# Moving the MLP's second product, the maximum pass, a norm and two tanh between the stages of a 16-batch attention and mixture-of-experts kernel

## The reference

```python
xn = layernorm(x)                                # plain, no gain
# branch 1: attention, a linear recurrence and an MLP
h  = layernorm(xn) * ln1_g + ln1_b
q, k, v = heads(h @ WQ + bQ), heads(h @ WK + bK), heads(h @ WV + bV)   # 16 heads of 8
scores = q @ k.T / sqrt(8); masked to 0 <= i - j < 128
ao = softmax(scores) @ v
states = scan(s = A * s + (h @ Bw)_t)
g  = sigmoid(h @ Wg + bg)
x1 = xn + g * (ao @ WO + bO) + (1 - g) * (states @ Cw)
s  = x1 + gelu(layernorm(x1) @ W1 + b1) @ W2 + b2
# branch 2: a mixture of 8 experts, 2 per token
xc = bfloat16(xn); nf = rmsnorm(xc) * norm_weight
w  = softmax over the two largest of (nf @ gate_weight.T + gate_bias)
y  = sum over experts e of w_e * expert_e(nf)    # clamped gated unit, then a second product
out = x + s * silu(xc + y)
```

## Time and profile before

| what | value |
|---|---|
| median of 3 runs | 1091.38 us (1089.91 to 1097.93) |
| time of the profiled execution | 1094.57 us |
| its span | 1092.8 us |
| TensorE matmul busy | 919.2 us, 84% of the span |
| VectorE busy | 782.5 us, 72% |
| ScalarE busy | 712.8 us, 65% |
| GpSimd busy | 501.8 us, 46% |
| mean granted TensorE clock | 0.925 of full speed |

### The profile page before, as it was taken

The page is one execution under the profiler, slowest core; times in us unless marked ns, Lnnn a source line. Parts: engine busy times, 40 slices in busy tenths (PEclk is TensorE's granted clock), DMA queues, the critical chain, the costliest instruction groups (busy, mean ns, idle before and its releaser), DMA issues.

```text
span 1092.8 us, 38402 instructions
## 1 busy us (share of the span) xinstructions
PE 919.2 (84%) x15864; PEld 561.7 (51%) x15864; DVE 782.5 (72%) x1990; ACT 712.8 (65%) x1126; POOL 501.8 (46%) x786
## 2 busy tenths in 40 slices
PE   2567898989889898988889898989888898978877
PEld 1333564646455464645555464645555464635435
DVE  4476777887877677888777777887777788656216
ACT  3205685858677595858768595867768585746645
POOL 6226355372736356273626456273635547152331
PEclk7557999999999899999999999998999999978869
DMA  5552414123332404224241503223241402310000
GB/s 108 129 118 67 93 46 105 32 94 64 100 62 75 90 27 108 50 90 62 92 75 53 112 24 109 52 90 63 75 93 36 111 17 99 58 31 6 25 1 10
DMA packets 85599, 75.24 MB, mean 69 GB/s; under 512 B 9329, under 2 KB 79154, under 8 KB 85426
## 3 DMA queue, kind: packets, MB, share of 16 engines
q1 hardware_dynamic: 83346, 72.00, 28.3%
q10 hardware_dynamic: 2080, 0.79, 0.3%
HBM read 36.33 MB, written 30.15 MB: 61 GB/s over the span
## 4 chain that ended last, share of the span: by engine, by line
PE 48%; DVE 25%; issue 13%; ACT 9%; POOL 2%; DMA 2%; DVEq 0%; SPq 0%; POOLq 0%; ACTq 0%
PE ps L558 8%; DVE mx L1074 6%; PE ps L500 6%; PE ps L690 5%; PE ps L750 5%; PE ps L711 5%; ACT pt L831 4%; PE ps L489 3%; DVE gc L1131 3%; PE ps L570 2%; DVE lin L1124 2%; PE ps L575 2%; ACT ot L836 2%; DVE junk L950 2%; PE ps L684 2%
## 5 line engine op out<-in xcount | busy, mean ns | idle before, releaser
L831 ACT ACTIVATE pt<-ps 128x1024 f32<-128x1024 f32 (+1 forms) x256 | 234.7, 917 | 212.5 <-PE ps L489 211.1
L1074 DVE TENSOR_REDUCE mx<-ps 128x2 f32<-128x320 f32 (+1 forms) x512 | 230.9, 466 | 110.6 <-PE ps L515 107.6
L1253 POOL TENSOR_SCALAR_AFFINE_SELECT pt<-pt 128x512 f32<-128x512 f32 x256 | 170.7, 669 | 264.6 <-ACT pt L831 264.3
L500 PE MATMUL ps<-kd,qz 48*32 48x160 bf16 (+1 forms) x4096 | 160.5, 241 | 66.6 <-DVE mx L1074 34.2
L489 PE MATMUL ps<-qz,kd 51*32 51x256 bf16 (+1 forms) x4096 | 183.5, 272 | 6.1 <-ACT pt L831 3.8
L558 PE MATMUL ps<-pt,va 128*32 128x256 f32 (+1 forms) x2048 | 159.8, 397 | 33.2 <-ACT ot L836 33.0
L500 PEld LDWEIGHTS ps<-kd,qz 48*32 48x32 bf16 x4096 | 72.7, 91 | 218.7 <-issue 121.3
L690 PEld LDWEIGHTS ps<-m,act_t 128*128 128x128 f32 x1024 | 126.8, 191 | 53.6 <-DVE act_t L1152 38.6
L690 PE MATMUL ps<-m,act_t 128*128 128x128 f32 x1024 | 143.2, 283 | 11.6 <-DVE act_t L1152 11.6
L1256 POOL TENSOR_SCALAR_AFFINE_SELECT pt<-pt 128x512 f32<-128x512 f32 x192 | 124.6, 649 | 0.0
L879 ACT ACTIVATE lin<-ps,mbias 128x512 f32<-128x512 f32 x128 | 87.7, 685 | 48.7 <-DVE act_t L1152 29.5
(11 more groups left out here) (158 smaller groups left out, 1672.7 us busy)
## 6 DMA issues: line engine op xcount, KB each, us to landing
qz<-qk_parts SPq DMA_DIRECT2D x32, 384.0 KB, 7.3
...
```

The lines of the kernel that those rows point to most:

```text
L500: nc.tensor.matmul(ps[QG * c:QG * (c + 1), 4 + par, w * pr:w * (pr + 1)], qz[q][rows, 2 * g + pr, P * i + QG * c:P * i + QG * (c + 1)], kd ...
L831: nc.scalar.activation(to, src, ACT.Exp, scale=SCALE).then_inc(exp_ok.sem, 1)
L1074: nc.vector.tensor_reduce(mx[:, i, HG * g + pr:HG * (g + 1):2], src, AX.X, ALU.max).then_inc(mx_ok.sem, 1)
L1253: sel1 = nc.gpsimd.affine_select(out=pt[:, s, :, 0:P], in_=pt[:, s, :, 0:P], compare_op=ALU.is_ge, fill=0.0, base=0, pattern=[[0, HG], [1, ...
```

## The change

`LEAD = 2`: a step n of the attention loop now computes the transposed scores of batch b at n, as before, but the maximum scores of batch b + 1 at n + 2. The maximum scores of steps 0 and 1 of a batch are computed at the end of the body before (`first_scores` on TensorE, `maxima` at the end of VectorE's body, behind z). nm is formed at step 14 and turned and copied at step 15, within the loops.

The MLP's second product isn't computed behind the last expert any more, but in the next body: half of it (`mlp_down`) behind the scores of step 0, half behind those of step 1, in front of the states product, which moves from step 0 to step 1. sres is formed in VectorE's step 5, `finish` moves from steps 1 and 3 to 7 and 9, and GpSimd's ob from step 2 to step 5.

`norm_x` moves from ScalarE to VectorE, as `(xl - mean) * r1`, ahead of z, so GpSimd's `minus` for it goes. `norm_h` moves from the end of ScalarE's body to steps 0 and 1 of the next. The two tanh move from the start of ScalarE's body behind the exponentials of steps 2 and 3. nmT's copy moves to step 15, which is ahead of the second tiny activation at step 16. The first two parts of `route_mix` move from steps 9 and 11 to 11 and 13.

```diff
-AT_STATES, AT_H0, AT_Q, AT_K, AT_U, AT_V, AT_G, AT_C = 0, 2, 4, 6, 8, 10, 12, 14
+LEAD = 2
+AT_STATES, AT_H0, AT_Q, AT_K, AT_U, AT_V, AT_G, AT_C = 1, 2, 4, 6, 8, 10, 12, 14
 AT_CAST, AT_SQ, AT_RS, AT_NF = 4, 6, 8, 10
 AT_H2 = 4
-MIX = (9, 11, 15, 16)
+MIX = (11, 13, 15, 16)
...
-        r1_step = signal("r1_step", 4)
+        r1_step = signal("r1_step", 2)
         r2_step = signal("r2_step", 4)
-        xn_ok = signal("xn_ok", NT)
+        xn_ok = signal("xn_ok", 2)
...
             def scores(b, q, n, half):
-                main, nxt = has(b), has(b + 1)
-                if main and half == 0:
-                    if n == 0:
+                main, nxt = has(b) and n < NCH, has(b + 1) and n + LEAD < NCH
+                if main:
+                    if n == 0 and half == 0:
                         pe.wait_ge(*done(stacks_in, b))
                         pe.wait_ge(*done(shift_in, b))
                         pe.wait_ge(*done(hid_ok, b - 1))
-                    if n >= 2:
+                    if half == 0 and n >= 2:
                         pe.wait_ge(*done(exp_ok, b, n - 1))
-                if main and half == 1 and n >= 1:
-                    pe.wait_ge(*done(exp_ok, b, n))
+                    if half == 1 and n >= 1:
+                        pe.wait_ge(*done(exp_ok, b, n))
                 if nxt:
-                    if n == 0 and half == 0:
-                        pe.wait_ge(*done(stacks_in, b + 1))
-                        pe.wait_ge(*done(gc_ok, b - 1, E))
-                    else:
-                        pe.wait_ge(*done(mx_ok, b + 1, 2 * n - 1 + half))
+                    maxima_free(b + 1, n + LEAD, half)
                 for pr in range(2):
                     if nxt:
-                        score(b + 1, 1 - q, n, half, pr)
+                        score(b + 1, 1 - q, n + LEAD, half, pr)
                     if main:
                         mm = score_t(b, q, n, 1 - half, pr)
                 if main and half == 1:
                     mm.then_inc(sT_ps.sem, 1)
                 if nxt:
-                    score_mask(n, half)
+                    score_mask(n + LEAD, half)
+            def maxima_free(b, n, half):
+                if n == 0 and half == 0:
+                    pe.wait_ge(*done(stacks_in, b))
+                    pe.wait_ge(*done(gc_ok, b - 2, E))
+                else:
+                    pe.wait_ge(*done(mx_ok, b, 2 * n - 1 + half))
+            def first_scores(b, q, n, half):
+                maxima_free(b, n, half)
+                for pr in range(2):
+                    score(b, q, n, half, pr)
+                score_mask(n, half)
...
+                def mlp_down(t):
+                    pe.wait_ge(*done(hid_ok, b - 1))
+                    for j in range(NJ):
+                        mm = nc.tensor.matmul(bank_t(6)[:, t], hid[:, j, P * t:P * (t + 1)], w2[:, j], start=j == 0, stop=j == NJ - 1)
+                    if t == NT - 1:
+                        mm.then_inc(w2_ps.sem, 1)
...
+                    if has(b - 1) and n < 2:
+                        mlp_down(2 * n)
+                        mlp_down(2 * n + 1)
                     if main and n == AT_STATES:
...
+                    if nxt and n == NCH - LEAD + 1:
+                        pe.wait_ge(*done(nm_step, b + 1))
+                        for t in range(NT):
+                            mm = nc.tensor.transpose(bank_bf(5)[0:NPART * H, P * t:P * (t + 1)], nm[:, t].rearrange("p r h -> p (r h)"), identb[:])
+                        mm.then_inc(nm_ps.sem, 1)
...
                     down(E - 1)
-                    for t in range(NT):
-                        for j in range(NJ):
-                            if t == 0:
-                                pe.wait_ge(*done(hid_ok, b, j + 1))
-                            mm = nc.tensor.matmul(bank_t(6)[:, t], hid[:, j, P * t:P * (t + 1)], w2[:, j], start=j == 0, stop=j == NJ - 1)
-                    mm.then_inc(w2_ps.sem, 1)
...
+                if nx2:
+                    if start(b, -2):
+                        all_set(pe)
+                        pe.wait_ge(masks_set.sem, N_MASKS)
+                    for n in range(LEAD):
+                        for half in range(2):
+                            first_scores(b + 2, q, n, half)
...
-                def norm_x(t):
-                    act.wait_ge(*done(r1_step, b + 3))
-                    act.wait_ge(*done(xn_copied, b + 1))
-                    nc.scalar.activation(xn[:, 1 - q, t], xl[:, 1 - q, t], ACT.Identity, bias=b1n[:, t:t + 1],
-                                         scale=r1[:, t:t + 1]).then_inc(xn_ok.sem, 1)
                 def norm_h(t):
-                    act.wait_ge(*done(r2_step, b + 3))
-                    act.wait_ge(*done(xn_ok, b + 3, t + 1))
-                    act.wait_ge(*done(hT_ps, b + 2))
-                    nc.scalar.activation(h0[:, t], xn[:, 1 - q, t], ACT.Copy, scale=r2[:, t:t + 1]).then_inc(h0_ok.sem, 1)
+                    act.wait_ge(*done(r2_step, b + 2))
+                    act.wait_ge(*done(xn_ok, b + 2))
+                    act.wait_ge(*done(hT_ps, b + 1))
+                    nc.scalar.activation(h0[:, t], xn[:, q, t], ACT.Copy, scale=r2[:, t:t + 1]).then_inc(h0_ok.sem, 1)
...
+                    if nx2 and n < 2:
+                        norm_h(2 * n)
+                        norm_h(2 * n + 1)
+                    if has(b - 1) and n == 2:
+                        soft_gate()
+                    if nxt and n == 3:
+                        mix_gate()
+                    if nxt and n == NCH - LEAD + 1:
+                        act.wait_ge(*done(nm_ps, b + 1))
+                        act.wait_ge(*done(shift_in, b))
+                        nc.scalar.activation(nmT[:], bank_bf(5)[0:NPART * H, :], ACT.Copy).then_inc(nmT_ok.sem, 1)
...
+            def norm_x(b, q, tiles):
+                if tiles[0] == 0:
+                    dve.wait_ge(*done(r1_step, b))
+                    dve.wait_ge(*done(xn_copied, b - 2))
+                for t in tiles:
+                    ts = nc.vector.tensor_scalar(xn[:, q, t], xl[:, q, t], mv[:, t, 0:1], r1[:, t:t + 1], ALU.subtract, ALU.mult)
+                ts.then_inc(xn_ok.sem, 1)
+            def maxima(b, n, pr):
+                g, i = n // NT, n % NT
+                w = WIN if i else P
+                dve.wait_ge(*done(s_ps, b, 2 * n + pr + 1))
+                if n == 0 and pr == 0:
+                    dve.wait_ge(*done(nm_step, b - 1))
+                src = bank(4 + pr)[:, 0:2 * w].rearrange("p (r k) -> p r k", r=2)
+                nc.vector.tensor_reduce(mx[:, i, HG * g + pr:HG * (g + 1):2], src, AX.X, ALU.max).then_inc(mx_ok.sem, 1)
...
+                        if nxt and n + LEAD < NCH:
+                            maxima(b + 1, n + LEAD, pr)
+                        if has(b - 1) and step == 5:
+                            dve.wait_ge(*done(w2_ps, b - 1))
+                            dve.wait_ge(*done(x1b_ok, b - 1))
+                            dve.wait_ge(*done(ob_ok, b - 2))
+                            nc.vector.tensor_tensor(sres[:], bank_t(6), x1b[:], ALU.add).then_inc(s_ok.sem, 1)
+                        if has(b - 1) and step in (7, 9):
+                            finish(b - 1, (step - 7) // 2)
...
-                    if nxt and n == NCH:
+                    if nxt and n == NCH - LEAD:
...
+                if nx3:
+                    norm_x(b + 3, 1 - q, (0, 1))
+                    norm_x(b + 3, 1 - q, (2, 3))
                 if main:
                     dve.wait_ge(*done(cb_ok, b))
                     dve.wait_ge(*done(xc_copied, b))
                     nc.vector.tensor_tensor(z[:], xcr[:], cb[:], ALU.add).then_inc(z_ok.sem, 1)
-                if main:
-                    dve.wait_ge(*done(w2_ps, b))
-                    dve.wait_ge(*done(x1b_ok, b))
-                    dve.wait_ge(*done(ob_ok, b - 1))
-                    nc.vector.tensor_tensor(sres[:], bank_t(6), x1b[:], ALU.add).then_inc(s_ok.sem, 1)
+                if nx2:
+                    if start(b, -2):
+                        dve.wait_ge(masks_set.sem, N_MASKS)
+                        route_rank(0)
+                    for n in range(LEAD):
+                        for pr in range(2):
+                            maxima(b + 2, n, pr)
...
-                    if n == 2 and has(b - 1):
+                    if n == 5 and has(b - 1):
...
-                    inv_root(r1[:], r1t[:], mv[:, :, 1], 1.0, r1_step, b + 3, 0, ((h0_ok, b + 2, None),))
-                    minus(n1[:], b1n[:], mv[:, :, 0], r1[:], r1_step, b + 3)
+                    inv_root(r1[:], r1t[:], mv[:, :, 1], 1.0, r1_step, b + 3, 0, ((xn_ok, b + 2, None),))
+                    pool.wait_ge(*done(r1_step, b + 3))
```

49 lines of the change are left out of this document (7 added, 42 removed).

## The result

| | before | after |
|---|---|---|
| median | 1093.97 us (1089.91 to 1097.93, 4 runs) | 1153.18 us (1150.76 to 1159.54, 4 runs) |
| profiled execution | 1094.57 us, span 1092.8 | 1150.76 us, span 1149.0 |
| mean granted TensorE clock | 0.925 | 0.961 |
| one undisturbed batch | 61.10 us | 64.99 us |

The ratio is 1.0551, with a 95% interval of 1.0488 to 1.0613: slower, 59 us by the medians, 56 by the two profiled executions. The forecast was 1141 us, with a range of 1092 to 1182 and a chance of 0.76 for slower.

What follows compares the result with a forecast made beforehand. TensorE bounds the batch end, VectorE the attention's middle, nothing is full in the tail. 2.65 + 0.4 + 0.5 = 3.55 us over 14 batches, less 1 each for batches 0 and 15: +48, 1141 us; own range 1122 to 1162, overall 1092 to 1182.

Steps and rivals of the forecast that it cites:

- The batch end: From last expert product to qr: first exponential 1.1 us earlier, but turning of h0 2.65 us late, making qr late.
- What would show it: Signs listed for the changed profile, such as TensorE waiting for third and fourth first-score halves, and a period near 64.7 us.
- The mix part moves into the stretch: +0.4: In VectorE's full stretch behind qr: the first mix part moves in and adds 0.4 us a batch.
- ob's term: GpSimd's ob addition at step 5, in the busier half: taken as 0, bounds 0 and 1.3 us.
- The tail: Last exponential to ot: 2.9 us instead of 2.0, as nmT's copy precedes the table load; +0.5 us, bounds -0.3 and +1.0.
- Norm on VectorE at 0: Ahead of z: four tensor_scalar fit into VectorE's 1.34 us wait for cb; cost 0, at most 0.4 us.
- Tanh, no new loads: On ScalarE: the two tanh moved behind exponentials bring no new table loads.
- Rival D: On ScalarE: tanh needs extra table loads, up to 5 us a batch, 1184 us; chance 0.04.
- The ends: Batch 0 with the prologue, and batch 15: each forecast at -1 us against the 14 full batches.
- B: VectorE's stretch shrinks by itself, giving back 2.5 of 3.55 us a batch: 1095 to 1104 us; chance 0.10.
- C: The attention's earlier opening sets the batch, so 1.1 us a batch is gained: 1077 us; chance 0.15.
- A, the clock: TensorE's clock falls at thinned tails and batch ends, slowing L750: 35 us more, 1176 us; chance 0.18.

Runs made afterwards that it cites:

- lead0: The changed kernel with LEAD = 0, so maximum scores run with the same step's transposed scores again: 1121.44 us, ratio 1.0255.
- states0: The changed kernel with the states product one step earlier, behind step 0 instead of step 1: 1144.10 us, ratio 1.0476.
- w2_back: The changed kernel with the MLP's second product at the batch end again, between the first scores of steps 0 and 1: 1161.16 us, ratio 1.0597.
- mix_back: The changed kernel with the first two mix parts at steps 9 and 11 again: 1152.05 us, ratio 1.0581.
- ob4_after: The changed kernel with GpSimd's ob at step 4 instead of 5: 1145.11 us, ratio 1.0497.
- combo family: The changed kernel with lead, states product, nm turning and nmT copy, and mix parts put back: 1087.09 us; with ob at step 4 too: 1085.78 us.
- nmt_late: The changed kernel with nmT's copy behind ScalarE's attention loop again, its transposes staying at step 15: 1146.61 us, ratio 1.0459.
- norm_act: The changed kernel with the norm of x on ScalarE again, with GpSimd's small steps for it: 1166.59 us, ratio 1.0715.
- w2_alone: The kernel before with only the MLP's second product moved to the next batch's steps 0 and 1, with sres, finish and ob: 1127.26 us, ratio 1.0336.

## Why the prediction was right, and where it was off

**The batch end: right, in its steps.** By the changed kernel's trace, counted from the last expert product's end (678.86): cb 0.04 behind it (0.05 predicted), z 0.67 (0.70), step 0's scores 2.55 (2.60), first exponential 3.32 (3.4), turning of h0 10.26 (10.35), qr 2.51 later than before (2.6 to 2.65). The third half waits 1.11 us for a maximum, as forecast; the other wait, 0.36, is that of step 0's first half for the third maximum, and the fourth half, which "What would show it" names, doesn't wait. The turning waits 1.03 for s1. lead0 and states0 back it: without the lead the turning comes 2.2 earlier, without the wait for s1 1.1. What the forecast did not see is how near the next waits are: w2_back covers one of them and gains 0.2, states0 removes 1.1 us and gains 0.6.

**"The mix part moves into the stretch: +0.4": the size was too small and the cause wrong.** The stretch grew by 0.84. exs and zs are in it now, with 0.32, but the product behind them is 0.25 shorter, and mix_back gives nothing back in the period. What grew is the squares, by 0.91. That is ob's term, for which I took 0 of a bound of 1.3, because GpSimd idles for 1.57 of 12 us in the stretch. That looked at GpSimd's time, and the cost was VectorE's: ob fell beside the squares, which slow down beside it. ob4_after returns 0.36 and not 0.8: the squares give back 0.67, but exs and the four nf take 0.35 and 0.36 more there, and cr 0.37 less. In the combo family the same edit returns 0.66, nearly all of the 0.72 that the stretch had grown there. So the forecast's sum came near the truth here partly by luck: one term was booked for another. The recorded "24 maxima before and after" is wrong too: from qr to the stretch's end stand 15 in both, and that the number is the same is all that the sum used.

**The tail: right.** 2.92 us from exponential to ot in the shown batch, 2.9 predicted; nmt_late returns 0.73 of the 0.9 in the undisturbed period. (The recorded 0.9 less 0.3 is 0.6; the sum took 0.5.)

**Norm on VectorE at 0: right.** The four take 1.11 us (bounds were 0.3 and 1.7) and z doesn't wait behind them. norm_act measures the other side: on ScalarE they would cost 0.26, the very 0.25 by which cb was forecast to be earlier.

**Tanh, no new loads: right.** The three table loads of a batch stand at the same places and count as before (16, 16 and 15); the two around the exponentials after:

```profile
L877 ACT ACT_TABLE_LOAD x16 | 20.5, 1283 | 0.3
...
L830 ACT ACT_TABLE_LOAD x15 | 19.2, 1283 | 0.3
```

(groups by line: busy us, mean ns, idle before.) Rival D is out.

**The sum.** 3.55 us a batch was forecast, and 3.89 came. Behind the product's end of the shown batch: qr 2.51 later, from qr to the last exponential 0.50 more (0.84 in the stretch less 0.34 in the lighter last steps, forecast at 0.4 less 0.3, with the 0.3 booked in the tail), from there to ot 0.90 more, together 3.91. From the attention's turned output to the product's end both take 21.22. The 14 periods between the z of batch 0 and that of batch 14 make 51.6 in the profiled executions, where the forecast had 50. The ends were wrong: the first z of VectorE stands at 153.38 and stood at 148.86, so the prologue and batch 0 cost 4.5 instead of -1. The first exponential there is in fact 0.9 earlier, 88.0 for 88.9. The time is lost in batch 0's own steps and in its tail, which the -1 left out: batch 0 has no product, but it has the wait of its maxima and s1, and its thin tail ran at the low clock. The stretch after, columns as in the earlier trace rows:

```profile
118.00:124.00 6.00, 4.32 (x80) 2.06 (x76) 2.78 (x7) 3.62 (x5) 3.10 (x6) 0.76 0.01 3
124.00:130.00 6.00, 5.28 (x40) 3.63 (x40) 1.10 (x4) 2.68 (x4) 0.48 (x1) 0.50 1.00 172
```

Before, the low level lasted from 119.6 to 123.0 only; here it lasts from 121.2 to 131.4. How the 4.5 divides stays open. The first z lies between 150.95 and 153.48 in the seven kernels with the lead and between 145.78 and 152.84 in the six without, and mix_back, which has no low stretch there, has it at 151.35, but so has w2_back, at 153.07. Batch 15 gained nothing (64.66 for 64.75), where -1 was forecast. 51.6 + 4.5 + 0.1 gives the span's 56.2. So of the 8 us by which this exceeds the forecast's 48, 6.6 are the ends' and 1.6 the periods'; what is left to 1153 are the medians, which stand 2.4 above this profiled execution after.

**The rivals.** B (the stretch catches up) and C (the opening sets the pace) are out: the stretch grew, and the earlier opening (0.94 to z, 1.2 to the product) didn't reach qr. A, the clock, is half right: the grant does fall at four batch ends of the changed kernel, at none before, and costs 1.5 to 1.65 us of the period each, and it falls in 5 tails of batches 1 to 15 (0.5 to 0.7 more where nothing else falls: 65.45 to 65.69). But the kernel before loses about as much, in 7 of its 15 tails, so that the recorded "most tails like this keep the full clock now" held for 8 of 15 only. The mean of the 14 whole periods rose from 62.16 to 65.84, by 3.7, hardly other than the undisturbed 3.89. So it isn't a cause of the difference between these two, and 35 us was far too much. In the profiled executions of norm_act and nmt_late, with eight batch ends each, and of w2_alone, with eleven low batches of 13, it is.

The Trainium skill (TensorE: Matmul & The Clock Gate, "What's actually happening") has activity release the clock and throttling as the default. Here the low grant comes behind a stretch in which TensorE was busy 1.44 and 0.71 of 2 us, which agrees, while other batch ends with the same waits kept the full clock.
